# Input transposes and the first head group's K and Q moved into the preceding batch's first layer

## The reference

```
q = (f + b_self) @ Wq + bq; k = concat(x + b_prev, f + b_self) @ Wk + bk; v = concat(x, f) @ Wv + bv
x = x + attention(q, k, v) @ Wo + bo      # 16 heads of 32; each row sees the x keys (masked) and its own f key
x = x + softmax((x + embed[stage]) @ f.T) @ f
h = relu(x @ W1[lang] + b1[lang]) @ W2[lang] + b2[lang]
x = x + layernorm(x + h) * gamma[lang] + beta[lang]
x = x + (x @ lora_A[rl].T) @ lora_B[rl].T + lang_embed[rl]
```

## Time and profile before

| | |
|---|---|
| median of 3 runs | 1389.57 us (1387.92 to 1389.87) |
| profiled execution | 1388.07 us, its span 1386.2 us |
| mean granted TensorE clock | 0.986 |
| TensorE busy | 1304.2 us, 94% |
| VectorE busy | 920.7 us, 66% |
| ScalarE busy | 879.9 us, 63% |
| GpSimd busy | 424.9 us, 31% |

### The profile page before, as it was taken

One profiled execution on the slowest core, in us unless ns is written; L12 is line 12 of the kernel. 1 busy time (PEld: TensorE's weight loads), 2 busy tenths in 40 slices (PEclk: granted clock), 3 DMA queues, 4 the chain that ended last, 5 costly groups with the idle time before them and its releaser, 6 DMA issues.

```text
span 1386.2 us, 20006 instructions
## 1 busy us (share of the span) xinstructions
PE 1304.2 (94%) x7049; PEld 563.4 (41%) x7049; DVE 920.7 (66%) x1600; ACT 879.9 (63%) x1857; POOL 424.9 (31%) x372
## 2 busy tenths in 40 slices
PE   6889999999999999899998999989999999999995
PEld 3332463325533255333543236432463325533252
DVE  4686468864697556975478745896468854598544
ACT  3697447883388744886458853687447883388731
POOL 4431044410533106430165102641044410533114
PEclk9999999999999999999999999999999999999996
DMA  5303012030221202220021301213012130220100
GB/s 172 88 23 102 1 54 71 30 102 16 56 67 41 77 32 51 57 86 31 31 70 47 109 1 38 71 39 110 1 54 68 33 101 14 56 70 25 63 1 31
DMA packets 62161, 75.82 MB, mean 55 GB/s; under 512 B 14378, under 2 KB 35174, under 8 KB 62062
## 3 DMA queue, kind: packets, MB, share of 16 engines
q1 hardware_dynamic: 62000, 74.53, 18.8%
q10 hardware_dynamic: 62, 0.01, 0.0%
HBM read 40.81 MB, written 8.40 MB: 35 GB/s over the span
## 4 chain that ended last, share of the span: by engine, by line
PE 63%; ACT 19%; DVE 14%; issue 3%; POOL 1%; DMA 0%; ACTq 0%; POOLq 0%
PE bank L456 23%; PE banks L456 12%; ACT banks L744 9%; DVE nmx L1018 9%; ACT big L796 7%; PE bank L1362 6%; PE banks L1346 6%; PE bank L1199 6%; PE banks L1280 3%; PE bank L1309 2%; PE bank L1372 1%; PE bank L1314 1%; DVE prod L1008 1%; PE bank L1336 1%; DVE y L1064 1%
## 5 line engine op out<-in xcount | busy, mean ns | idle before, releaser
L744 ACT ACTIVATE banks<-banks,nmx 128x512 f32<-128x512 f32 x512 | 340.5, 671 | 55.6 <-DVE nmx L1018 53.2
L1018 DVE TENSOR_REDUCE nmx<-banks 128x1 f32<-128x512 f32 x512 | 325.9, 684 | 70.2 <-PE banks L1280 69.1
L796 ACT ACTIVATE big<-banks 128x1024 f32<-128x1024 f32 x256 | 247.3, 1022 | 43.6 <-PE banks L1346 42.5
L456 PE MATMUL bank<-fT,w_hi 128*128 128x512 f16 x768 | 246.9, 383 | 1.2 <-issue 1.1
L1280 PE MATMUL banks<-KQ 97*128 97x512 f16 x512 | 155.3, 385 | 38.6 <-ACT banks L744 36.5
L530 POOL TENSOR_TENSOR big<-x,b2r 128x512 f32<-128x512 f32 x32 | 40.6, 1269 | 412.2 <-DVE x L945 372.2
L1346 PE MATMUL banks<-KQ 98*128 98x512 f16 x512 | 141.0, 382 | 13.4 <-ACT big L796 8.4
L456 PE MATMUL bank<-fT,w_lo 128*128 128x512 f16 x384 | 147.3, 384 | 0.0
L491 POOL TENSOR_TENSOR half<-qk,ones 128x512 f16<-128x512 f32 x64 | 66.5, 1040 | 227.9 <-ACT qk L724 206.6
L1362 PE MATMUL bank<-big,V 128*32 128x512 f32 x1024 | 136.4, 605 | 0.0
L456 PEld LDWEIGHTS bank<-fT,w_hi 128*128 128x128 f16 x768 | 75.5, 98 | 93.3 <-issue 18.0
(11 more groups left out here) (149 smaller groups left out, 1968.2 us busy)
## 6 DMA issues: line engine op xcount, KB each, us to landing
KQ<-half SPq DMA_DIRECT2D x384, 64.0 KB, 2.0
tiles_in<-in_x_dram SPq DMA_DIRECT2D x32, 256.0 KB, 7.2
tiles_in<-in_fside_BxSxS_dram SPq DMA_DIRECT2D x32, 256.0 KB, 2.8
x<-in_x_dram SPq DMA_DIRECT2D x8, 1024.0 KB, 6.0
out_dram<-x SPq DMA_DIRECT2D x32, 256.0 KB, 2.0
w<-in_L_cond_W_dram SPq DMA_DIRECT2D x16, 256.0 KB, 4.6
b2r<-in_L_cond_b_dram SPq DMA_DIRECT2D x8, 256.0 KB, 4.4
gr<-in_L_cond_gamma_dram SPq DMA_DIRECT2D x8, 256.0 KB, 5.3
```

What stands on the lines that cost most here:

```text
L456: mm = eng.matmul(out_ap, pairs[n][0], pairs[n][1], start=(first and n == 0), stop=(last and n == len(pairs) - 1))
L744: ins = eng.activation(bank(step, i)[:, j % 2, :], bank(step, i)[:, j % 2, :], ACT.Exp, bias=nmx[:, t, h:h + 1], accum_out=esum[:, t, h:h ...
L796: eng.activation(big[:, n % 2, 2 * u:2 * u + 2, :], bank(step)[:, :, :], ACT.Exp).then_inc(read(step), 1)
L1018: eng.tensor_reduce(nmx[:, t, h:h + 1], bank(step, i)[:, j % 2, :], AX_X, ALU.max, negate=True).then_inc(max_done, 1)
```

## The change

- In all batches but the last, the layer's table `ORDER_L1` now takes the `NIN` steps earlier and after them, between the later steps of the layer, `IN` 4 to 7 and the thirds of `K` 0 and `Q` 0 of the next batch (the set `EARLY`), ahead of `PV1` 2 and 3. `mid` with a tail starts with `KS` 0 (the splits `HALF` of K 0 and Q 0 first).
- `OPEN[0]`, now counted from the first third of `KS` 0, is 8; before, 16 from `Q` 0, which is 15 from that third.
- Banks: `NIN` moves to the pairs 4 and 6, `IN` to banks 2 and 3. `plan_banks` now counts the uses along the order of the whole program.
- Waits: K 0 waits on TensorE until the last two `NIN` are read.

```diff
+def parts(step):
+    return [("PART", n, step) for n in range(PARTS - 1)] + [step]
...
-    slots = [("IN", NT), ("IN", NT + 1), ("PART", 0, ("K", 0)), ("IN", NT + 2), ("PART", 1, ("K", 0)),
-             ("IN", NT + 3), ("K", 0)] + parts(("Q", 0)) + parts(("KS", 0))
+    slots = ([] if tail else [("IN", NT), ("IN", NT + 1), ("PART", 0, ("K", 0)), ("IN", NT + 2), ("PART", 1, ("K", 0)),
+                              ("IN", NT + 3), ("K", 0)] + parts(("Q", 0))) + parts(("KS", 0))
...
-    opens = [slots.index(("Q", g)) + OPEN[g] for g in range(NG)]
+    opens = [slots.index(("Q", g) if g else ("PART", 0, ("KS", 0))) + OPEN[g] for g in range(NG)]
...
+    if tail:
+        out += [("HALF", "K", 0), ("HALF", "Q", 0)]
...
-OPEN = (16, 13, 13, 13)
+OPEN = (8, 13, 13, 13)
...
-ORDER_L1 = [("WOP", 1), ("WOP", 2), ("WO", 0), ("WO", 1), ("WOP", 3), ("X1T", 0), ("X1T", 1), ("WO", 2),
-            ("WO", 3), ("S1", 0), ("X1T", 2), ("S1", 1), ("X1T", 3), ("P1T", 0), ("S1", 2),
-            ("P1T", 1), ("PV1", 0), ("S1", 3), ("P1T", 2), ("PV1", 1), ("NIN", 0), ("P1T", 3), ("NIN", 1),
-            ("PV1", 2), ("NIN", 2), ("NIN", 3), ("PV1", 3)]
...
-NIN_BANKS = (3, 0, 3, 1)
...
+EARLY = set([("IN", NT + n) for n in range(NT)] + parts(("K", 0)) + parts(("Q", 0)))
...
+ORDER_L1 = ([("WOP", 1), ("WOP", 2), ("WO", 0), ("WO", 1), ("WOP", 3), ("X1T", 0), ("X1T", 1), ("WO", 2),
+             ("WO", 3), ("NIN", 0), ("S1", 0), ("NIN", 1), ("X1T", 2), ("NIN", 2), ("S1", 1), ("NIN", 3), ("X1T", 3),
+             ("P1T", 0), ("S1", 2), ("P1T", 1), ("PV1", 0), ("S1", 3), ("IN", NT), ("P1T", 2), ("PV1", 1),
+             ("IN", NT + 1), ("IN", NT + 2), ("P1T", 3), ("IN", NT + 3)]
+            + parts(("K", 0)) + parts(("Q", 0)) + [("PV1", 2), ("PV1", 3)])
...
+        home.update({("WO", t): (4, 6)[t // 2], ("X1T", t): t % 2, ("P1T", t): t % 2, ("S1", t): 2 + t % 2,
+                     ("PV1", t): (4, 6)[t % 2], ("NIN", t): (4, 6)[t % 2], ("IN", NT + t): 2 + t % 2})
+        home.update({(kind, t): 2 for kind in ("X2T", "HID", "ADP", "X3T", "LOW", "LORA")})
...
+            for step in ORDER_L1:
+                give(step, i + 1 if step in EARLY else i)
+            for step in order_mid(True, True):
+                give(step, i if step in ADAPTER_STEPS else i + 1)
...
+                    if step in EARLY:
+                        mid(True, True, i, [step])
+                        continue
...
+                    if step == ("K", 0):
+                        wait_read(eng, ("NIN", NT - 2), b - 1)
+                        wait_read(eng, ("NIN", NT - 1), b - 1)
```

More of the change, by code:

```diff
@@ L168, in plan_banks, with home_banks @@
+def home_banks():
+    home = {}
     n = m = 0
     for step in order_mid(False, True):
[L170 to L173, removed]
+        if step[0] in ("Q", "K", "KS", "VS", "V"):
+            home[step] = n % 2
             n += 1
         elif step[0] == "SMAX":
[L176 removed]
+            home[step] = (4, 6)[m % 2]
             m += 1
[L178 to L179 removed]
+    home.update({("MROW",): 4, ("SROW",): 6, ("PREPB",): 2, ("PREPA",): 3})
@@ L182, in plan_banks, with order_attention @@
+    return home
+def order_attention():
+    order = []
     for g in range(NG):
-        give(2, ("NORMS", g))
-        give(3, ("SELFW", g))
-        give(g % 2, ("PV", g))
         for k in range(NT):
[L187 to L205, removed]
+            order += [("ST", g, k, 0), ("ST", g, k, 1)]
+        order += [("PV", g), ("NORMS", g), ("SELFW", g)]
+    return order + [("PREPB",), ("PREPA",)]
 ADAPTER_BANKS = (2, 3, 0, 1)
@@ L212, in order_last @@
     cut = ORDER_L1.index(("PV1", 1)) + 1
-    return ([step for step in ORDER_L1[:cut]]
+    return ([step for step in ORDER_L1[:cut] if step not in EARLY and step[0] != "NIN"]
             + [("X2T", 0), ("P1T", 3), ("HID", 0), ("X2T", 1), ("PV1", 2), ("ADP", 0), ("HID", 1), ("SQ", 0),
@@ L219, in order_last, with plan_banks, give @@
                ("LORA", 2), ("LOW", 3), ("LORA", 3)])
[L222 to L233, removed]
-ADAPTER_STEPS = set(order_mid(True, False))
-BEFORE = {k: NIN_BANKS.count(k) + (k == 2) for k in USES}
-LAST = plan_last()
+ADAPTER_STEPS = set(order_mid(True, False))
+def plan_banks():
+    home = home_banks()
+    where, count = {}, {k: int(k == 2) for k in (0, 1, 2, 3, 4, 6)}
+    def give(step, b, k=None):
+        if step in home:
+            k = home[step] if k is None else k
+            where[step, b] = (k, count[k])
+            count[k] += 1
+    for n in range(NT):
+        give(("NIN", n), -1)
+    for step in order_mid(False, True):
+        give(step, 0)
+    for i in range(B):
+        for step in order_attention():
+            give(step, i)
+        if i == B - 1:
+            for step in order_last():
+                give(step, i, ADAPTER_BANKS[step[1]] if step in ADAPTER_STEPS else None)
+        else:
+            for step in ORDER_L1:
+                give(step, i + 1 if step in EARLY else i)
+            for step in order_mid(True, True):
+                give(step, i if step in ADAPTER_STEPS else i + 1)
+    return home, where
+HOME, WHERE = plan_banks()
 def build_program(nc, x, f, len_, stage_, lang_, rlang_, Wq, bq, Wk, bk, Wv, bv, Wo, bo, b_prev, b_self,
@@ L1198, in transpose4 @@
                 for d in range(4):
-                    mm = eng.transpose(bank(step, b)[:, d * P:(d + 1) * P], src[:, d * P:(d + 1) * P], ident[:, :])
+                    mm = eng.transpose(tile_of(step, b)[:, d * P:(d + 1) * P], src[:, d * P:(d + 1) * P], ident[:, :])
                 mm.then_inc(done(step, b), 1)
```

23 lines of the change are left out of this document (8 added, 15 removed).

## The result

The changed kernel takes 1415.05 us, the median of 4 runs (1413.95 to 1420.11). The kernel before, on the same chip, takes 1388.74 us (1387.61 to 1389.87, 4 runs). The ratio is 1.020, with a 95% interval of 1.0184 to 1.0215: 26 us slower. The profiled execution's span is 1412.4 us against 1386.2. The forecast was 1415; the total was met by luck in part: its periods were forecast 7 us too long in all and its first stage 6 us too short, and the two misses cancel.

The account below looks back on a forecast made before the run. TensorE's own work plus its stalls in the maxima, 7 us per batch, was taken as the bound. Terms 0.9 + 0 + 2.1 + 0.3 + 0.6 gave 3.9 us per batch, 27 in seven: 1415 us, range 1394 to 1432.

Parts of the forecast that it names:

- Part 1: First layer: four input transposes (1.74 us) and K, Q of group 0 (5.2 us) move in from `mid`; sum 0.
- Part 2: First layer: stalls of 0.7 us at `IN` 7 and some 0.2 at `PV1` 0; cost 0.9, between 0 and 2.
- Part 3: Stretch of the maxima in `mid`: 57.0 us of work, stalls 7.3 us against 7.0 before, taken as 0.
- one pace of 1.80: Stretch of the maxima: each `SMAX` takes 1.80 us, so a group of eight needs 12.6; group stalls together 6.3.
- Part 4: End of `mid`: waits at `MROW` 0.7, `LOW` 2 0.7, `LORA` 3 0.6, two of 0.05; 2.1 us, between 0.6 and 3.5.
- Part 5: Start of the attention: second score bank pair and first exponential wait behind `LORA` 3's addition; 0.3 us (0 to 1.5).
- Part 6: Normalisers after `SROW`: VectorE's group 0 starts 1.6 us later, `NORMS` 2 is 0.9 late; cost 0.6 (0 to 1).
- partly in slack: Normalisers: `NORMS` 2's 0.9 us lateness falls partly in slack left by the exponentials, leaving 0.6 us.
- The first stage: Stage with no layer ahead: `SMAX` 0 asked for 6 us earlier with the same transfers; 0, or 3 either way, once.
- The rival of a faster ring: Stretch of the maxima keeps a 1.59 us pace, stalls fall to 2.0; 1378 us (1368 to 1385), chance 0.20.
- The rival of a bound VectorE: Group 0 of the maxima: normalisation costs 3 to 4 us more, 7 us per batch; 1437 us, chance 0.14.
- 3.9 + 3: Cost per batch by the port-lock rule if GpSimd is always busy beside VectorE's six normalisation steps; 3.9 if idle.

Follow-up runs that it names:

- experiment 8: The change with experiment 7's packing, first-stage `SMAX` opened after 15 thirds, layer order K 0, `IN` 7, `PV1` 2, Q 0, `PV1` 3: 1406.5 us, ratio 1.014.
- experiment 9: The change with first-stage `SMAX` opened after 15 thirds and layer order K 0, `IN` 7, `PV1` 2, Q 0, `PV1` 3, adapter list untouched: 1403.36 us, ratio 1.0117.
- experiment 7: The change with five free places taken out of the adapter list from `X3T` 0 on, none ahead of the first normalisation: 1418.63 us, ratio 1.022.
- experiment 3: The change with five free places taken out of the adapter list, its start included, so `SROW` comes two thirds before the end: 1424.31 us, ratio 1.025.
- experiment 10: The kernel before, with the maxima of the first stage alone opened 2 thirds later: 1382.27 us against 1386.8 us, ratio 0.9965.
- experiment 5: The kernel before, with `SROW` alone moved to the end of `mid`, adapters and opening unchanged: 1400.86 us, ratio 1.010.

## Why the prediction was right, point by point

- **Total.** 26.3 us of span against 27 forecast, with parts that err both ways: a period 2.87 instead of 3.9 (seven times 1.0 too much), the first stage 6.4 instead of 0. That these two cancel is luck. By its periods alone the change would cost 20 us, which the range (1394 to 1432) also holds.
- **Part 1, work moved.** Right: the layer had nothing free. From attention to first `SMAX` 10.46 us of work left and the time fell by 9.6.
- **Part 2, waits in the layer.** Forecast 0.9; measured 1.1 (0.8 at `IN` 7, 0.3 at `PV1` 0), in the two places named. Experiments 8 and 9 took 0.8 of it back in those periods in which the transfers weren't late.
- **Part 3, the stretch.** Forecast 0 and 63 to 65 us; measured 0.4 won and 63.5 us. The sum of stalls, 7.3 against 7.0, was 6.5 against 6.9. The reason given for the sum was only half right. By one pace of 1.80 the four groups were to stall 0.4, 2.3, 1.0 and 2.6 us; by the same count they stalled 1.5, 1.3, 0.7 and 2.1, with 0.9 between them, so the sum came out and its parts didn't. VectorE's load was taken to be in the way of a faster ring; its `NORM` work became 5 us a batch cheaper here (39 us in all by the page) and the ring hardly noticed. What the runs add: five empty places fewer in the adapter list cost 1.8 us of stall (experiment 7), so the stretch follows from how adapter steps, their own bank and the maxima alternate.
- **Part 4, the end of `mid`.** Forecast 2.1 with `MROW` 0.7, `LOW` 2 0.7, `LORA` 3 0.6; measured 2.4 with 0.7, 0.7 and 0.65. This is the term that sets the result: it alone is larger than what the stretch won. Its waits stand in the trace, but no run took it back: with the list packed (experiments 3 and 7) 1.7 and 0.9 us of these stalls went and 2.7 and 1.8 new ones came in the stretch. That `mid` in this order has to stall some 9 us wherever the adapters stand is a rival that these runs don't exclude.
- **Part 5, into the attention.** Forecast 0.3; measured 0.1.
- **Part 6, normalisers.** Forecast 0.6; measured 0. They are ready 1.5 us later, but `NORMS` on TensorE come 0.1 later (14.78 against 14.65 us after the attention's start). VectorE's first copy behind them comes 0.4 later in the first period and 1.4 in the next, and TensorE never waits for it. The step that failed is "partly in slack": it was wholly in slack.
- **The first stage.** Forecast 0, within 3; measured 6.4. The step that failed is "what it waits there it mostly gives back in the stalls that follow". The prediction took the transfers' 2.0 us each and a start of `SMAX` 6 us earlier, but not that the twelve transfers of a group leave the queue one after another, 0.65 us apart, and that in the kernel before the first `SMAX` already began as the last of them landed. So the whole move forward became a wait: it was 7.28, at the end of which the clock is low, and a second of 3.50 followed. None of it was given back.
- **The rival of a faster ring** (1378) fell with the stretch: its point of decision was 3.9 us won, and 0.4 came. **The rival of a bound VectorE** (1437) was 0.14. In the change most of the moved steps found GpSimd idle; in experiment 3 they didn't, and TensorE waited 2.02 us in group 0, but set beside experiment 7 no more than 0.5 us a period is left for it, where the rival had 3 to 4. The Trainium skill (SBUF — State Buffer, "Who interferes with whom") states that of the two engines the one that issues first holds the shared ports for its whole instruction and the other is blocked, and that `tensor_reduce` never contends. The traces agree: steps of 0.16 and 0.17 with GpSimd idle; of 1.12 and 1.19 beside it, each ending 0.02 us after GpSimd's operation; of 0.53 where GpSimd had 0.5 us left; and reductions of 685 ns in both kernels. So the price of a step is what is left of GpSimd's operation when it starts, and neither the full 1.20 nor a mean. The 1 us that the prediction took for six such steps was too much for most of them. Its "3.9 + 3" by the rule was also not what its own row gives: six steps at 1.04 more are 6.2 us of VectorE's time.

What stays open: whether the stretch can be had at 63 us with an end of 8, that is, with `SROW` early and the adapters neither packed nor last. `SROW` ahead of `LORA` 3 with an unpacked list would tell; it needs other buffers than the adapters', and it wasn't tried.

## What to carry to other kernels

A stage whose work moves elsewhere leaves its partners behind: when projections leave `mid`, the steps that they spaced and covered (here the adapters at its end) come to stand in a row, and that chain's waits must be summed beside the gain. A start that is moved forward is worth nothing where a slower ring, a transfer or a busy engine sets what comes second; look at the third use of the ring, not at the first. Look also at how long before its use the last transfer lands: in experiments 8 and 9 1.0 us of margin was not enough, because some transfer at times took 1.2 to 1.7 us longer than the others. And look at every program part that shares the changed table, the one that runs once too.

## What the runs showed of the hardware

- A fall of VectorE's busy time by 39 us (4%) without any change of its work: the steps of 128x2 cost from 0.16 to 1.2 us by what GpSimd does meanwhile, and end as its operation ends. Busy time is here partly waiting, and a move of a few us changes it.
- Transfers of 64 KB on one queue were issued 0.65 us apart and took 2.0 us each from issue to landing, but not all: in experiment 9 the slowest of a group's first twelve took 3.2 to 3.7 us in five periods of seven, in the change 2.9 to 3.2 in three.
- TensorE's clock after waits. In the rows after 7.28 and 3.33 us without work the clock was at the lower of its two levels (two matmuls drawn at 1.03 and 1.04 us instead of 0.60); after 2.08 us in experiment 10 it was not. After 2.02 us in experiment 3 it fell in two stages of seven (0.60 over the next 4 us) and stayed at 1.00 in the others; after 1.54 and 0.68 in experiment 5 likewise (0.58 or 1.00). Where it fell, the stall cost 1.4 to 1.6 us more than itself. So equal periods of one program need not be equally long once each holds a wait of this size. The longest in a period of the kernel before is 1.65 us, and there all seven last 166.5; what decides stays open.
